# Cross-attention on one Trainium2 core: evener steps, a ring of four value chunks, output rows in one piece in the third step

## The chip, the cores and the metric

The kernel runs on one core of one Trainium2 chip. Its time is the device time of one execution in microseconds (us); lower is better. Engines are named as in the profile: PE is TensorE's matmul stream and PEld its weight loads, DVE is VectorE, ACT ScalarE, POOL GpSimd, SP SyncE, which issues most DMAs here.

## The reference

A pre-norm decoder layer on `x` of 32 x 112 x 512, float32, in three parts that each add to `x`: windowed self-attention, cross-attention to a context of 32 x 375 x 256, and an expert layer. The change is in the cross-attention alone:

```python
q = (layernorm(x) @ Wq)            # 16 heads of 128
k, v = ctx @ Wk, ctx @ Wv          # 8 key/value heads of 128, each used by two query heads
scores = einsum('bhtd,bhsd->bhts', q, k) / sqrt(128)
attn = softmax(where(mask, scores, -inf))
out = einsum('bhts,bhsd->bhtd', attn, v)
x = x + out @ Wo                   # 2048 -> 512
```

## The kernel before, in words

`cross_attention` does the heads in two halves (`HALVES`), so there are 64 pairs of a half and a batch, called batches 0 to 63 here (`b`); 0 to 31 are the first half. A batch has four steps (`g` 0 to 3, one key/value head and its two query heads each), 256 steps in all (`i = 4b + g`). Every product is made of matmuls on split numbers: a value is kept as a high part and a rest, and a product is three matmuls for each 128 of depth (high x rest, rest x high, high x high). So every tile that PE makes is read from PSUM twice: ACT copies the high part (`fill` at L1191, `probsT` at L1198, `out` at L1207), then DVE subtracts it and keeps the rest (`fill` at L1272, `probsT` at L1302, `out` at L1311).

In a step PE does, in this order (`@block.tensor`): the scores S of the step; the early fills, above all K, the keys of the same head for batch b+1; the product P of probabilities and values of two steps before; the late fills; the transposes T of the probabilities of the step before; the last late fill. The fills besides K are C (the context transposed, two per batch, first half only; it is written to DRAM and loaded again in the second half), V (the values, three chunks V0, V1, V2 of 128, 128 and 120 context rows), Q (the queries of four batches, eight fills, two in each step of every fourth batch, those with b mod 4 = 3) and O (the output rows, 24 matmuls for one tile of 128 rows, into which 28 of the 32 batches of a half bring one). Before the change C stands in step 3 ahead of P, all of V in step 1 around T, and O in step 2 ahead of P. All fills, O too, take PSUM banks in turn from `BANKS = 3`: a fill waits until DVE is through with the fill three places before it (`pe.wait_ge(fill_done, ...)` in `fill`).

The softmax of a step runs: DVE masks the scores and takes the maximum (`maxima`, L1295), POOL makes the bias (L1165), ACT the exponentials (L1215), DVE the inverse of the sum (`inverses`, L1320, L1323), POOL multiplies (L1171), PE transposes. ACT does in a step: weight splits, the K fill and C, the exponentials, a split of `xT` (input of Q, in the batches with b mod 4 = 1), `out`, `probsT` among the other fills. DVE: the mask row (step 0), `maxima`, weight splits, K and C, `inverses`, the `xT` split, the addition of the output rows (`add`, L1278), `out`, fills, `probsT`. Both engines take these in the written order, and a wait of one holds all behind it.

The context of a batch, the mask rows and the tiles of the residual are loaded by SP in one written order, and so are the weights, whose second half is loaded while the first is still in use (`splits_at` says in which steps they are split).

Of the kernel before, what the change touches and what calls it, by code (L numbers as in the profile page):

```python
# [16 lines left out]
P = 128  # L17
# [842 lines left out]
def cross_attention(nc, B, T, S, h2T, ctx, mask, Wq, Wk, Wv, Wo, base, mid, result):  # L860
# [19 lines left out]
    QUAD = 4  # L880
    T4 = QUAD * T
# [3 lines left out]
    RING = 2 * P  # L885
    SCALE = float(1.0 / np.sqrt(D))
    mdt = mask.dtype
    assert B * T % RING == 0 and B % QUAD == 0 and SE > S and T * 2 <= RING
# [9 lines left out]
    def early_fills(i):  # L898
        b, g = divmod(i, G)
        out = [("K", b + 1, g)] if b + 1 < NB else []  # L900
        if g == 3 and b + 2 < B:
            out += [("C", b + 2, 0), ("C", b + 2, 1)]
        if g == 2 and b in TILE_OF:
            out.append(("O", TILE_OF[b], 0))
        return out

    def late_fills(i):
        b, g = divmod(i, G)
        out = [("V", b, c) for c in range(NKC)] if g == 1 else []
        if b % QUAD == QUAD - 1 and b + 1 < NB:  # L910
            out += [("Q", b // QUAD + 1, 2 * g + h) for h in range(2)]
        return out

    def before_transposes(i):
        return late_fills(i)[:-1]

    def behind_transposes(i):
        return late_fills(i)[-1:]

    HEAD = [("C", 0, 0), ("C", 0, 1)] + [("K", 0, g) for g in range(G)] + [("C", 1, 0), ("C", 1, 1)] + \  # L920
           [("Q", 0, h) for h in range(H)]
    TAIL = ("O", TILE_OF[NB], 0)
    ORDER = HEAD + [f for i in range(STEPS) for f in early_fills(i) + late_fills(i)] + [TAIL]
    PLACE = {f: n for n, f in enumerate(ORDER)}
    assert len(PLACE) == len(ORDER)
    HALVED = {f: n for n, f in enumerate([f for f in ORDER if f[0] != "O"])}
    BANKS = 3
# [14 lines left out]
    PIECES = {"k": CC, "v": CC, "q": KC, "o": H // 2}  # L942
    FIRST_SPLITS = [("k", 0, n) for n in range(CC)], [("q", 0, n) for n in range(KC)], [("v", 0, n) for n in range(CC)]

    def splits_at(i):
# [3 lines left out]
        if b == B - 8 and g < CC:  # L949
            return [("k", 1, g)]  # L950
        if b == B - 3:
            return [("q", 1, g)]
        if i == G * B:
            return [("v", 1, n) for n in range(CC)]
        if b == B + 1:
            return [("o", 1, g)]
# [10 lines left out]
    def x_piece(i):  # L967

        b, g = divmod(i, G)
        return b // QUAD + 1 if b % QUAD == 1 and b // QUAD + 1 < NB // QUAD else None  # L970
# [3 lines left out]
    with ExitStack() as stack:  # L974
# [5 lines left out]
        wk = sb("wk", [P, HALVES, 2, CC, G * D], F32R)  # L980
# [5 lines left out]
        ctxn = sb("ctxn", [P, 2, NKC, CD])  # L986
        ctxT = sb("ctxT", [P, 2, 2, CC, SE], F32R)
        kT = sb("kT", [P, 2, G, SE], F32R)
        v = sb("v", [P, 2, NKC, G * D], F32R)
# [4 lines left out]
        mraw = sb("mraw", [T, 2, S], mdt)  # L994
# [27 lines left out]
        fill_ready, fill_hi, fill_done = sem("fill_ready"), sem("fill_hi"), sem("fill_done")  # L1022
        base_in = [sem(f"base_in{n}") for n in range(2)]
        stored = [sem(f"stored{n}") for n in range(2)]

        def weight(piece):

            kind, half, n = piece
            return [{"k": lambda: wk[:, half, a, n, :], "v": lambda: wv[:, a, n, :], "q": lambda: wq[:, a, n, :],
                     "o": lambda: wo[:, a, 2 * n:2 * n + 2, :]}[kind]() for a in (HI, LO)]  # L1030

        def weight_source(piece):
            kind, half, n = piece
            if kind in "kv":
                return (Wk if kind == "k" else Wv)[n * P:(n + 1) * P, half * G * D:(half + 1) * G * D]
# [1056 lines left out]
```

## Time and profile before

| | |
|---|---|
| median of 3 runs | 2684.8 us (2684.68 to 2687.51) |
| the profiled execution | 2685.35 us |
| its span | 2683.7 us |
| mean granted TensorE clock | 0.957 |
| PE busy | 2482.7 us (93%) |
| DVE busy | 1733.0 us (65%) |
| ACT, POOL busy | 1241.2, 1030.1 us |

The cross-attention takes from about 462 to 2395 us of the span. The page's busy shares are means over three stages; the views by line and the timeline tell more. In a timeline row stand the start, how long the run of equal instructions lasted, engine, line, operation and tiles; in brackets the engine's idle time before it and who ended it. Runs of matmuls overlap by the depth of the pipeline, so the distance between two starts, not the length, is what a run takes.

### The profile page before, as it was taken

Reading aid. Unit: us, or ns where it says so; the run is one execution under the profiler, and the core shown is the slowest. Engines: PE = TensorE matmul, PEld = TensorE weight load, DVE = VectorE, ACT = ScalarE, POOL = GpSimd, SP = SyncE. Lnnn points to the kernel's source line nnn. Section 1 sums busy time; section 2 is a strip of 40 time slices with the busy share of each in tenths; the row PEclk is TensorE's granted clock in tenths of the full one; section 3 lists DMA queues with packets and bytes.
Section 4 is the critical chain, followed back from the end, with each engine's and each line's share of the span. In section 5 each row is a group of like instructions: output and inputs, shape, how many; then the busy total and the mean of one; then the engine's idle time right before and its main releaser. Section 6 shows DMA issues by size and latency. Waiting matters only on the chain. (4 is left out here: it accounts for less than half of the span.)

```text
span 2683.7 us, 46237 instructions
## 1 busy us (share of the span) xinstructions
PE 2482.7 (93%) x14850; PEld 2257.6 (84%) x14851; DVE 1733.0 (65%) x4899; ACT 1241.2 (46%) x3183; POOL 1030.1 (38%) x1424
## 2 busy tenths in 40 slices
PE   6899897799999999999999999999999999979488
PEld 5888886788989898889989898898989888869376
DVE  7878886565575657566575756656565665644466
ACT  4555553454454545445454545445454454522211
POOL 4334443243343434334353534334343343431422
PEclk9999998899999999999999999999999999975699
DMA  8322332412122112212121211111111111122654
GB/s 256 95 71 84 96 108 89 162 50 66 62 75 66 62 54 74 74 52 83 52 91 58 88 55 53 54 41 55 51 57 54 53 55 41 41 72 70 220 178 129
DMA packets 108892, 217.87 MB, mean 81 GB/s; under 512 B 20336, under 2 KB 48720, under 8 KB 108416
## 3 DMA queue, kind: packets, MB, share of 16 engines
q1 hardware_dynamic: 103440, 188.42, 21.9%
q0 software_dynamic: 5040, 16.58, 1.7%
q10 hardware_dynamic: 224, 10.49, 1.2%
q8 instruction: 104, 1.70, 0.3%
q14 instruction: 84, 0.69, 0.1%
HBM read 134.57 MB, written 91.36 MB: 84 GB/s over the span
## 5 line engine op out<-in xcount | busy, mean ns | idle before, releaser
L1171 POOL TENSOR_SCALAR x_probs<-x_probs,x_inv 112x376 f32<-112x376 f32 x512 | 639.3, 1258 | 273.6 <-DVE x_inv L1323 273.6
L1165 POOL TENSOR_SCALAR x_bias<-x_top 112x1 f32<-112x1 f32 x512 | 129.1, 252 | 871.8 <-DVE x_top L1295 864.9
L1215 ACT ACTIVATE x_probs<-x_probs,x_bias 112x376 f32<-112x376 f32 x512 | 307.0, 603 | 105.2 <-POOL x_bias L1165 104.7
L1380 PE MATMUL x_ps_o<-x_pT,x_v 128*128 128x224 f32 (+1 forms) x2304 | 310.3, 279 | 43.2 <-DVE x_pT L1302 42.5
L1380 PEld LDWEIGHTS x_ps_o<-x_pT,x_v 128*128 128x128 f32 (+1 forms) x2304 | 288.0, 192 | 69.6 <-DVE x_pT L1302 61.5
L1380 PE MATMUL x_ps_f<-x_xT,x_wq 128*128 128x448 f32 x1536 | 339.3, 371 | 4.5 <-issue 4.5
L1380 PE MATMUL x_ps_f<-x_wo,x_oT 128*128 128x512 f32 x1344 | 315.7, 391 | 1.0 <-DVE x_oT L1311 1.0
L1380 PE MATMUL x_ps_s<-x_kT,x_qT 128*112 128x376 f32 x1536 | 314.6, 340 | 1.5 <-DVE x_top L1295 1.5
L1380 PE MATMUL x_ps_f<-x_ctxT,x_wk 128*128 128x376 f32 x1536 | 306.4, 335 | 1.9 <-DVE x_ctxT L1272 1.9
L1380 PEld LDWEIGHTS x_ps_f<-x_xT,x_wq 128*128 128x128 f32 x1536 | 282.4, 189 | 26.5 <-issue 4.7
L1380 PEld LDWEIGHTS x_ps_f<-x_wo,x_oT 128*128 128x128 f32 x1344 | 252.6, 189 | 50.0 <-issue 1.2
L1380 PE MATMUL x_ps_f<-x_wv,x_ctxT 128*128 128x512 f32 (+1 forms) x1152 | 290.7, 399 | 0.0
L1380 PEld LDWEIGHTS x_ps_f<-x_ctxT,x_wk 128*128 128x128 f32 x1536 | 269.4, 189 | 2.8 <-issue 1.6
L1295 DVE CUSTOM_DVE_ANT_0 x_probs<-x_ps_s,x_mrow 112x376 f32<-112x376 f32 x512 | 259.0, 543 | 11.1 <-DVE x_mrow L1283 11.1
L1380 PEld LDWEIGHTS x_ps_s<-x_kT,x_qT 128*112 128x112 f32 x1536 | 253.4, 175 | 10.0 <-issue 1.8
L1191 ACT ACTIVATE x_kT<-x_ps_f 128x376 fp32r<-128x376 f32 x256 | 124.1, 485 | 275.7 <-PE x_ps_f L1380 275.3
L1380 PEld LDWEIGHTS x_ps_f<-x_wv,x_ctxT 128*128 128x128 f32 (+1 forms) x1152 | 206.1, 187 | 43.1
L1302 DVE TENSOR_TENSOR x_pT<-x_ps_t,x_pT 128x336 fp32r<-128x336 f32 x512 | 234.2, 499 | 0.3 <-ACT x_pT L1198 0.3
L1207 ACT ACTIVATE x_oT<-x_ps_o 128x224 fp32r<-128x224 f32 (+6 forms) x352 | 93.7, 294 | 264.0 <-PE x_ps_o L1380 264.0
L1272 DVE TENSOR_TENSOR x_qT<-x_ps_f,x_qT 128x448 fp32r<-128x448 f32 x128 | 80.0, 625 | 208.7 <-ACT x_qT L1191 208.7
L1198 ACT ACTIVATE x_pT<-x_ps_t 128x336 fp32r<-128x336 f32 x512 | 202.1, 452 | 0.3 <-PE x_ps_t L1443 0.2
L1272 DVE TENSOR_TENSOR x_v<-x_ps_f,x_v 128x512 fp32r<-128x512 f32 (+1 forms) x192 | 132.5, 691 | 91.3 <-ACT x_v L1191 91.0
(186 smaller groups left out, 3799.5 us busy)
## 6 DMA issues: line engine op xcount, KB each, us to landing
x_ctxs<-x_ctxT SPq DMA_DIRECT2D x32, 752.0 KB, 3.8
x_ctxT<-x_ctxs SPq DMA_DIRECT2D x32, 752.0 KB, 4.3
x_xT<-h2T SPq DMA_DIRECT2D x16, 896.0 KB, 5.0
m_rows<-slots SPq DMA_DIRECT2D x35, 258.0 KB, 3.0
slots<-w_blank SPq DMA_DIRECT2D x8, 1032.0 KB, 5.2
x_ctxn<-in_ctx_dram SPq DMA_DIRECT2D x32, 256.0 KB
m_hn<-in_L_ffn_W_dram SPq DMA_DIRECT2D x32, 256.0 KB
w_xa<-in_x_dram SPq DMA_DIRECT2D x32, 224.0 KB, 3.3
```

Source lines behind the costliest of these rows:

```text
L1165: pool.tensor_scalar(bias[:, m:m + 1], top[:, m:m + 1], -0.1 * NEG, -SCALE, ALU.max, ALU.mult) \
L1171: pool.tensor_scalar(probs[0:T, m, 0:SE], probs[0:T, m, 0:SE], inv[:, m:m + 1], None, ALU.mult).then_inc(normed, 1)
L1191: act.activation(dst[HI], src, ACT.Copy).then_inc(fill_hi, 1)
L1198: act.activation(pT[:, HI, :, h * T:(h + 1) * T], ps_t[h][:, 0:NKC * T].rearrange("p (c t) -> p c t", c=NKC), ACT.Copy).then_inc(pT_hi, 1)
L1207: last = act.activation(oT[:, HI, 2 * g:2 * g + 2, at:at + t1 - t0], rows[:, :, t0:t1], ACT.Copy)
L1215: act.activation(probs[0:T, m, 0:SE], probs[0:T, m, 0:SE], ACT.Exp, bias=bias[:, m:m + 1], scale=SCALE, accum_out=total[:, m:m + 1]).then_ ...
L1272: dve.tensor_tensor(dst[LO], src, dst[HI].bitcast(F32), ALU.subtract).then_inc(fill_done, 1)
L1295: dve.tensor_tensor_reduce(out=probs[0:T, m, 0:SE], in0=ps_s[h][0:T, 0:SE], in1=mrow[:, i // G % 2, :], scale=1.0, scalar=-3.0e38, op0=ALU ...
L1302: dve.tensor_tensor(pT[:, LO, :, h * T:(h + 1) * T], ps_t[h][:, 0:NKC * T].rearrange("p (c t) -> p c t", c=NKC), pT[:, HI, :, h * T:(h + 1 ...
L1380: last = pe.matmul(out, w, r, start=m == 0, stop=m == len(jobs) - 1)
```

## The change

- Fills take their PSUM bank from two (`BANKS = 2`); the output rows leave the ring and have a bank of their own, `ps_r`, with counters of their own (`rows_ready`, `rows_added`). They still come in one piece in step 2 (`ROWS_AT = {2: [(0, H)]}`).
- V0 of batch b+1 moves to step 3 of batch b, so `v` becomes a ring of four chunks (`VRING`); V1 and V2 stay in step 1. C moves to step 2 (first of the two) and step 3, behind P.
- ACT does the exponentials first in a step, then K; DVE does `maxima`, then `inverses`, then K, then `out`, and only then `add`. The mask row moves to the end of step 1, the splits of weights and of `xT` to the end of a step; the `xT` splits now stand in steps 1 and 2 of the batches with b mod 4 = 1 and 2.
- One buffer instead of two for the context and the raw mask, and for `Wk`, which is cut in four pieces by heads instead of two by depth; `oT` holds three tiles of rows instead of two. SP's order is rewritten: in the head, `Wo` is loaded behind the second mask row, whose load waits for DVE's first `mask_row`; in the second half it is loaded behind the wait for V2 of batch 33.
- In the head, C of batch 1 moves between the fourth and the fifth Q fill, and V0 of batch 0 stands at the end.

```diff
-    RING = 2 * P
+    VRING = NKC + 1
+    RING = 3 * P
...
     def early_fills(i):
         b, g = divmod(i, G)
-        out = [("K", b + 1, g)] if b + 1 < NB else []
-        if g == 3 and b + 2 < B:
-            out += [("C", b + 2, 0), ("C", b + 2, 1)]
-        if g == 2 and b in TILE_OF:
-            out.append(("O", TILE_OF[b], 0))
-        return out
+        return [("K", b + 1, g)] if b + 1 < NB else []
 
     def late_fills(i):
         b, g = divmod(i, G)
-        out = [("V", b, c) for c in range(NKC)] if g == 1 else []
+        out = []
+        if g >= 2 and b + 2 < B:
+            out.append(("C", b + 2, g - 2))
+        if g == 3 and b + 1 < NB:
+            out.append(("V", b + 1, 0))
+        if g == 1:
+            out += [("V", b, c) for c in range(1, NKC)]
...
-    BANKS = 3
+    BANKS = 2
...
+    ROWS_AT = {2: [(0, H)]}
...
@@ scalar
                 for i in range(STEPS):
-                    for p in splits_at(i):
-                        split(p)
+                    exps(i)
                     for f in early_fills(i):
-                        if f[0] != "O":
-                            fill(f)
-                    exps(i)
-                    if x_piece(i) is not None:
-                        split_x(x_piece(i), i % G)
+                        fill(f)
...
@@ vector
                     maxima(i)
-                    for p in splits_at(i):
-                        split(p)
+                    inverses(i)
                     for f in early_fills(i):
-                        if f[0] != "O":
-                            fill(f)
-                    inverses(i)
...
                     if i >= 2:
                         out(i - 2)
+                    for tile, h0, h1 in row_parts(i):
+                        if h1 == H:
+                            add(tile)
```

PE, step 3 of a batch of the first half. The digit behind `x_ps_f` is the bank; `x_wk` marks K, `x_ctxn` C, `x_wv` V, `x_ps_s` S, `x_ps_o` P and `x_ps_t` T. Before:

```order
L1380 MATMUL x_ps_s0<-x_kT,x_qT 112x376 x3
L1380 MATMUL x_ps_s1<-x_kT,x_qT 112x376 x3
L1380 MATMUL x_ps_f2<-x_ctxT,x_wk 128x376 x6
L1392 MATMUL x_ps_f0<-x_ident,x_ctxn 128x128 x2
L1392 MATMUL x_ps_f0<-x_ident,x_ctxn 128x120
L1392 MATMUL x_ps_f1<-x_ident,x_ctxn 128x128 x2
L1392 MATMUL x_ps_f1<-x_ident,x_ctxn 128x120
L1380 MATMUL x_ps_o<-x_pT,x_v 128x224 x9
L1443 MATMUL x_ps_t0<-x_ident,x_probs 128x112 x3
L1443 MATMUL x_ps_t1<-x_ident,x_probs 128x112 x3
```

The same step after the change:

```order
L1410 MATMUL x_ps_s0<-x_kT,x_qT 112x376 x3
L1410 MATMUL x_ps_s1<-x_kT,x_qT 112x376 x3
L1410 MATMUL x_ps_f1<-x_ctxT,x_wk 128x376 x6
L1410 MATMUL x_ps_o<-x_pT,x_v 128x224 x9
L1422 MATMUL x_ps_f0<-x_ident,x_ctxn 128x128 x2
L1422 MATMUL x_ps_f0<-x_ident,x_ctxn 128x120
L1482 MATMUL x_ps_t0<-x_ident,x_probs 128x112 x3
L1482 MATMUL x_ps_t1<-x_ident,x_probs 128x112 x3
L1410 MATMUL x_ps_f1<-x_wv,x_ctxT 128x512 x6
```

One C has gone to the step before, the other stands behind P, and V0 ends the step in the bank that K had in the same step.

DVE, step 3 of the same batch. `x_kT`, `x_ctxT`, `x_v` are the rests of K, C, V; `x_sums` is `add`, `x_oT` is `out`, `x_pT` is `probsT`; `x_probs,x_top` and the `x_top` behind it are `maxima`, `x_total` and `x_inv` are `inverses`. Before:

```order
L1295 ISA x_probs,x_top<-x_ps_s,x_mrow 112x376
L1295 ISA x_top 112x1
L1295 ISA x_probs,x_top<-x_ps_s,x_mrow 112x376
L1295 ISA x_top 112x1
L1272 TENSOR_TENSOR x_kT<-x_ps_f,x_kT 128x376
L1272 TENSOR_TENSOR x_ctxT<-x_ps_f,x_ctxT 128x376 x2
L1320 TENSOR_SCALAR x_total<-x_total 112x1
L1323 RECIPROCAL x_inv<-x_total 112x1
L1320 TENSOR_SCALAR x_total<-x_total 112x1
L1323 RECIPROCAL x_inv<-x_total 112x1
L1311 TENSOR_TENSOR x_oT<-x_ps_o,x_oT 128x2x112
L1302 TENSOR_TENSOR x_pT<-x_ps_t,x_pT 128x3x112 x2
```

The end of step 2, from `add` on, and step 3 up to K after the change:

```order
L1307 TENSOR_TENSOR x_sums<-x_ps_r,x_sums 128x512
L1302 TENSOR_TENSOR x_ctxT<-x_ps_f,x_ctxT 128x376
L1331 TENSOR_TENSOR x_pT<-x_ps_t,x_pT 128x3x112 x2
L1324 ISA x_probs,x_top<-x_ps_s,x_mrow 112x376
L1324 ISA x_top 112x1
L1324 ISA x_probs,x_top<-x_ps_s,x_mrow 112x376
L1324 ISA x_top 112x1
L1349 TENSOR_SCALAR x_total<-x_total 112x1
L1352 RECIPROCAL x_inv<-x_total 112x1
L1349 TENSOR_SCALAR x_total<-x_total 112x1
L1352 RECIPROCAL x_inv<-x_total 112x1
L1302 TENSOR_TENSOR x_kT<-x_ps_f,x_kT 128x376
```

K has moved from ahead of `inverses` to behind them; `add`, which stood ahead of `out` in step 2, now stands behind it, with a C between it and `probsT`.

## Rows read from the trace of the kernel before

**Rows 1.** The page, part 1, the line of TensorE.

```profile
PE 2482.7 (93%) x14850; PEld 2257.6 (84%) x14851; DVE 1733.0 (65%) x4899; ACT 1241.2 (46%) x3183; POOL 1030.1 (38%) x1424
```

**Rows 2.** Waits of PE, 545 to 1420 us.

```profile
PE x_ps_o L1380 <- DVE x_pT L1302: 17.8, 23, 1.9
```

**Rows 3.** Waits of PE, 1420 to 2360 us.

```profile
PE x_ps_o L1380 <- DVE x_pT L1302: 18.6, 29, 1.8
```

**Rows 4.** Timeline of PE, end of batch 16 and start of 17.

```profile
1005.99 1.26 PE L1380 MATMUL x_ps_s<-x_kT,x_qT 128*112 128x376 f32 x6
...
1008.12 0.81 PE L1392 MATMUL x_ps_f<-x_ident,x_ctxn 128*128 128x128 f32 x6
1008.69 1.24 PE L1380 MATMUL x_ps_o<-x_pT,x_v 128*128 128x224 f32 x9
...
1010.28 1.27 PE L1380 MATMUL x_ps_s<-x_kT,x_qT 128*112 128x376 f32 x6
...
1012.42 1.17 PE L1380 MATMUL x_ps_o<-x_pT,x_v 128*128 128x224 f32 x9
...
1013.94 1.25 PE L1380 MATMUL x_ps_s<-x_kT,x_qT 128*112 128x376 f32 x6
...
1017.37 1.27 PE L1380 MATMUL x_ps_o<-x_pT,x_v 128*128 128x224 f32 x9 [1.16 <-DVE x_pT L1302]
1018.47 2.96 PE L1380 MATMUL x_ps_f<-x_wv,x_ctxT 128*128 128x512 f32 x12
```

**Rows 5.** Timeline of DVE, the same stretch.

```profile
1007.29 0.54 DVE L1295 CUSTOM_DVE_ANT_0 x_probs<-x_ps_s,x_mrow 112x376 f32<-112x376 f32 x1
...
1008.84 0.55 DVE L1272 TENSOR_TENSOR x_kT<-x_ps_f,x_kT 128x376 fp32r<-128x376 f32 x1 [0.53 <-ACT x_kT L1191]
1009.30 0.99 DVE L1272 TENSOR_TENSOR x_ctxT<-x_ps_f,x_ctxT 128x376 fp32r<-128x376 f32 x2
...
1012.85 0.55 DVE L1295 CUSTOM_DVE_ANT_0 x_probs<-x_ps_s,x_mrow 112x376 f32<-112x376 f32 x1 [0.17 <-DVE x_mrow L1283]
...
1015.56 0.63 DVE L1266 TENSOR_TENSOR x_xT<-x_xT 128x448 fp32r<-128x448 f32 x1
1016.11 0.38 DVE L1311 TENSOR_TENSOR x_oT<-x_ps_o,x_oT 128x224 fp32r<-128x224 f32 x1
1016.41 0.91 DVE L1302 TENSOR_TENSOR x_pT<-x_ps_t,x_pT 128x336 fp32r<-128x336 f32 x2
```

**Rows 6.** Timeline of ACT, the same stretch.

```profile
1008.32 0.49 ACT L1191 ACTIVATE x_kT<-x_ps_f 128x376 fp32r<-128x376 f32 x1 [1.56 <-PE x_ps_f L1380]
...
1014.97 0.56 ACT L1184 ACTIVATE x_xT<-x_xT 128x448 fp32r<-128x448 f32 x1
```

**Rows 7.** Groups by line: costs of single DVE operations, mean ns.

```profile
L1278 DVE TENSOR_TENSOR x_sums<-x_ps_f,x_sums 128x512 f32<-128x512 f32 x56 | 38.8, 692 | 187.9 <-PE x_ps_f L1380 187.9
```

**Rows 8.** Timeline of PE and DVE, step 3 of batch 15, a batch with Q fills.

```profile
976.29 1.19 PE L1380 MATMUL x_ps_s<-x_kT,x_qT 128*112 128x376 f32 x6
...
977.61 0.54 DVE L1295 CUSTOM_DVE_ANT_0 x_probs<-x_ps_s,x_mrow 112x376 f32<-112x376 f32 x1
```

**Rows 9.** Stretches of PE: us, busy (x), granted clock, DMA share, GB/s.

```profile
1487.00:1520.00 33.00, 28.64 (x193) 1.00 0.31 105
2355.00:2396.00 41.00, 34.14 (x182) 0.88 0.03 12
```

**Rows 10.** Timeline of DVE, first step.

```profile
511.90 1.29 DVE L1262 TENSOR_TENSOR x_wv<-x_wv 128x512 fp32r<-128x512 f32 x2
...
513.63 0.55 DVE L1295 CUSTOM_DVE_ANT_0 x_probs<-x_ps_s,x_mrow 112x376 f32<-112x376 f32 x1 [0.19 <-DVE x_mrow L1283]
```

**Rows 11.** Issue to landing of `Wo`, second half (tile x_wo, 1470 to 1520).

```profile
DMA to landing us min/median/max: 6.8/7.2/7.6
```

**Rows 12.** The same, first half (400 to 560).

```profile
DMA to landing us min/median/max: 10.6/10.9/11.3
```

**Rows 13.** The page, part 6: KB each, median us to landing.

```profile
x_ctxT<-x_ctxs SPq DMA_DIRECT2D x32, 752.0 KB, 4.3
```

More of the change, by code:

```diff
@@ L1007, in cross_attention @@
         ps_o = bank("ps_o")
+        ps_r = bank("ps_r")
         ps_f = [bank(f"ps_f{n}") for n in range(BANKS)]
@@ L1248, in _ @@
                         fill(f)
+                    if x_piece(i) is not None:
+                        split_x(*x_piece(i))
+                    for p in splits_at(i):
+                        split(p)
                 out(STEPS - 2)
@@ L1361, in _ @@
                         fill(f)
+                    if i % G == 1 and i // G + 1 < NB:
+                        mask_row(i // G + 1)
+                    if x_piece(i) is not None:
+                        split_x(*x_piece(i))
+                    for p in splits_at(i):
+                        split(p)
                 out(STEPS - 2)
@@ L1401, in fill @@
                                 pe.wait_ge(fill_done, until(("C", at, 1)))
-                        last = product(out[:, 0:SE], [(wk[:, half, a, c, n * D:(n + 1) * D], ctxT[:, at % 2, b_, c, :])
+                        last = product(out[:, 0:SE], [(wk[:, a, c, n * D:(n + 1) * D], ctxT[:, at % 2, b_, c, :])
                                                       for c in range(CC) for a, b_ in PASSES])
@@ L1414, in fill, with rows @@
                                                       for c in range(KC) for a, b_ in PASSES])
[L1415 to L1421 removed]
+                    last.then_inc(fill_ready, 1)
+                def rows(tile, h0, h1):
+                    if h0 == 0:
+                        weights("o", tile // TILES)
+                        pe.wait_ge(o_lo, G * (last_batch(tile) + 1))
+                        if tile:
+                            pe.wait_ge(rows_added, tile)
+                    slot = tile * P % RING
+                    for h in range(h0, h1):
+                        for a, b_ in PASSES:
+                            last = pe.matmul(ps_r[:], oT[:, a, h, slot:slot + P], wo[:, b_, h, :],
+                                             start=h == 0 and (a, b_) == PASSES[0],
+                                             stop=h == H - 1 and (a, b_) == PASSES[-1])
+                    if h1 == H:
+                        last.then_inc(rows_ready, 1)
                 def scores(i):
@@ L1463, in _ @@
                         fill(f)
+                    for tile, h0, h1 in row_parts(i):
+                        rows(tile, h0, h1)
                     if i >= 2:
@@ L1474, in _ @@
                 pv(STEPS - 1)
-                fill(TAIL)
+                rows(HALVES * TILES - 1, 0, H)
 def expert_ffn(nc, B, T, x2, wg, W, b, slots, out):
```

186 lines of the change are left out of this document (99 added, 87 removed).

## The prediction

> **What bounds the kernel now.** The first thing to read is the page's first part: PE is busy for 2482.7 of 2683.7 us [rows 1]. So the change can gain only what PE waits, or lose what it makes PE wait. It adds no matmul and takes none away. The list of waits of PE says what the cross-attention waits for: P for the probabilities that DVE halves last (L1302), 17.8 us in the first half and 18.6 us in the second [rows 2, 3]. Thirdly I read the timeline of a short stretch to see how these waits come about [rows 4 to 6]. PE takes 4.29 us for a step 3 (1005.99 to 1010.28) and 3.66 us for a step 0 (to 1013.94). DVE takes 5.56 us from the maxima of that step 3 to those of the step 0 (1007.29 to 1012.85), and its next `probsT` ends at 1017.32. Two short steps in a row let DVE fall behind, and the P of step 1 starts 1.16 us late, at 1017.37. The long steps (V, output rows) let DVE catch up. In three of four batches something of this is left; where the Q fills make every step long, nothing is.
>
> **The change part by part.** *Evening.* V0 lengthens step 3 by 1.45 us on PE (half of the 12 matmuls of 2.96 us, with their tail) [rows 4] and takes them from step 1. That is what the wait in step 1 needs, and taken alone it removes it.
>
> *How late DVE comes into step 3.* In the trace DVE starts the maxima at 1007.29, 1.30 us behind the start of the scores [rows 4, 5]. Now `add` (0.69 us, 0.62 of it not overlapped by its neighbour) [rows 7] no longer runs while DVE waits for ACT's `out`, but after it, and a C (0.99 us for two, 0.47 each) follows [rows 5]. The maxima start at 1007.29 + 0.62 + 0.47 = 1008.38. PE starts the scores later by one C only (half of 1008.69 - 1008.12), at 1006.27 [rows 4]. The lag grows from 1.30 to 2.1 us.
>
> *When K is free.* ACT now does K after both exponentials. In step 0 of the trace ACT is through with them and starts its next operation at 1014.97, 2.12 us behind DVE's maxima (1012.85) [rows 5, 6]. From ACT's start of K to DVE's start of K it is 0.52 us (1008.32, 1008.84), DVE takes 0.55, and PE follows 0.05 later (1017.32, 1017.37) [rows 4 to 6]. So K's bank is free 3.24 us behind the maxima: 1011.62.
>
> *The new wait.* The ring has two banks. In the first half step 3 fills them with K, C, V0, so V0 needs K's bank. PE is through with S, K, P, C and T of the step 4.29 us less one C after its start, and wants V0 at 1006.27 + 4.29 - 0.28 = 1010.28. V0 waits 1.3 us. Nothing of this is hidden: the scores of step 0 are queued behind V0 on PE, and DVE and POOL can't gain on it. In batches with b mod 4 = 1 or 2 an `xT` split (0.55 us, 1015.56 to 1016.11) [rows 5] now closes step 2 and delays the maxima: 1.9 us. With Q fills DVE comes 1.32 us behind PE into step 3 (976.29, 977.61) [rows 8], and V0 directly follows C: K is free at 4.56 us of the step, V0 wants to start behind scores and K (2.13), P (1.10, from 1017.37 to 1018.47) and one C (0.29) [rows 4], at 3.5: 1.1 us. Four batches: 1.3 + 1.9 + 1.9 + 1.1 = 6.2 us, and batches 2 to 29 are seven times four: **43 us**.
>
> *The old wait.* V0 ends 1.45 us after its release, DVE halves it and is 1.3 us behind PE in step 0; one short DVE step is now 4.2 us: 2.64 to the start of K, 0.46 for K, 0.30 for `out` (1016.11 to 1016.41), 0.83 for `probsT` (0.91 with its tail) [rows 5]. P of step 1 wants 3.66 + 2.14 = 5.8 us behind the start of step 0 [rows 4], the probabilities are there at 1.3 + 4.2 = 5.5. The old wait goes: **-17.8 us** [rows 2]. V2 in step 1 also takes K's bank. It wants it behind 2.13, P 1.10, V1 1.4 and T 0.5, 5.1 us into the step; DVE is 1.3 + 4.2 - 3.66 = 1.9 behind by then and frees it at 1.9 + 3.24: under 0.1 us, times 28 some **2 us**. In batches 9, 17 and 25 no output rows lengthen step 2, so on a lag of 2.1 us comes a DVE step of 4.7 against 3.95 on PE; P of step 3 wants its probabilities at 2.13 and has them at 2.8: 3 x 0.7 = **2 us**. First half: 43 - 17.8 + 2 + 2 = 29, **+29 us**.
>
> *Second half.* No C is made, so V0 follows K, and its bank is the one of K of step 2, long free. No V0 wait. But K has left the shadow in which DVE waited for the exponentials, and V0 adds 0.6 us of DVE to step 3. DVE enters step 3 with a lag of 1.9 us and needs 4.8 and 4.2 for steps 3 and 0, together 10.9; P of step 1 wants its probabilities at 5.1 + 3.66 + 2.14 = 10.9. So the wait is near 0.1 us, 0.65 where an `xT` split came before, and V2 waits 0.1 more: 0.2, 0.25, 0.8 and 0 in the four kinds of batches, 7.5 times 1.25 = 9 us. The four batches without rows add 1 us each: 13. Before it was 18.6 less the 4.4 of a stretch with weight splits (33.00 - 28.64) [rows 3, 9]: **-1 us**.
>
> *Weights at the half.* `Wo` now queues on SP behind the wait for V2 of batch 33, behind the copy of `ctxT` (752 KB, 4.3 us to land) [rows 13]. It lands 7.2 us after its issue if the copy doesn't hold it [rows 11], 11.5 if it does. DVE reaches the first split some 7 us after V2 (a lag of 2.1, a step of 4.2, an `xT` split of 0.55). With an issue or two ahead of it in the queue `Wo` is there after 8.5 to 12.5 us, so ACT and DVE stand 1.5 to 5.5 us; I take **+3 us**. The pieces of `Wk` come ahead of long steps: 0, covered by the output rows; at worst 3 us.
>
> *The head.* V0 needs the split of `Wv`, which DVE ends at 513.19 [rows 10]; the C that filled a gap adds 0.57. V0 then ends at 515.2, ACT and DVE halve it (0.6, 0.69), the mask row takes 0.44, and the first maxima start at 516.95 and not 513.63 [rows 7, 10]: 3.3 us. `Wo` is issued only when the mask row is done, and lands 7.2 us later [rows 11], 524.2; ACT is ready for it at 520.1. These 4.1 us nothing hides, since PE has only short steps there. With 0.5 us for K out of the shadow in three steps: **+9 us**. Bounds: the landing may be 10.9 us [rows 12], 13 in all; or only a few us in an empty queue, 4 in all. In these bounds lies also the 512-byte cut of `Wk`, two issues more ahead of the first context.
>
> *No cost.* `ps_r` makes `add` free of the ring, but the next fill doesn't wait for it before either. One buffer for context and mask: each is loaded at least a step 0 and a step 1 (3.7 + 6.7 us) ahead. Fewer `out`s are cut in two by the longer `oT`: a gain of some 3 us at most.
>
> **Sum.** 29 - 1 + 3 + 9 = 40 us on the profiled execution's own 2685.35: 2725.4 us. That execution is 0.5 us over the median of the runs, 2684.8, so I say 2725.
>
> The Trainium skill (Perfetto Trace Analysis, Optimizing Tensor Performance) has independent matmul groups rotate through different PSUM banks, so that the evacuation of one overlaps the next; it speaks against three banks made two. It gives no price; the sum by the rule alone is a V0 and V2 wait wherever the evacuation is late, which is what the rows give here.
>
> **Rivals.** *A: the evening works (faster).* K's bank is free in time, since PE is held elsewhere or ACT gets K in between. Then the waits of both halves go but for 2 us, -17.8 - 14.2 + 2 = -30, and the 12 us for head and half stay: 2667 us. It decides at a release of K less than 2.0 us behind the maxima, when the lag is 2.1. For it: the exponentials start earlier than before. Against it: ACT's order is fixed, and 2.12 us alone pass before it may touch K [rows 5, 6]. 0.11.
>
> *B: the wait is there but half as long*, because DVE's lag into step 3 stays 1.3 us (`add` and C find gaps): V0 waits 0.5, 1.1, 1.1 and 1.1 us in the four kinds, 27 us for 43: 2709 us. With a cheap head, 2704. For it: DVE has idle time between the exponentials. 0.13, inside the range.
>
> *C: gains and costs cancel*: V0 waits some 0.6 us in every batch, 17 us for 43, and the head costs 4 for 9: 2694 us, or a little less. 0.05.
>
> *D: TensorE's clock falls.* In the last steps, with 6.9 us of waits in 41, the granted clock is 0.88, and 1.00 in a stretch with 4.4 us in 33 [rows 9]. If each V0 wait cost the next 3.66 us step the lower level (1.2 for 2.4 GHz), 28 x 3.66 = 102 us more: 2827 us. Against it: waits of up to 1.9 us [rows 2] leave the clock at full level. The Trainium skill (TensorE: Matmul & The Clock Gate, A second HAM failure mode: psum-queue depth-cycling) tells of a kernel whose clock went up and down from short idle times while it cycled through PSUM banks; by that rule the rival would come true, and the trace so far doesn't agree. 0.03.
>
> **How the numbers follow.** The forecast has 0.68, its own range is 2710 to 2746: the V0 wait by 0.3 us either way is 8 us, the head -5 to +4, the half -1 to +3, `Wk` to +3. With B the range is 2696 to 2746; it leaves out A, most of C, D and the ends. Within 0.2%, 5 us, is about what a measurement of this kernel can tell from no change. Faster: A and a hundredth of C, 0.12; same: most of C, 0.04; slower: the forecast, B and D, 0.84.
>
> **What would show it.** In the profile after: a wait of PE for K's rest ahead of V0 (x_ps_f, released by DVE x_kT) in each batch up to 29, 1.1 to 1.9 us, and none in batches 32 to 63; the wait of P for the probabilities nearly gone in the first half and about the same in the second; DVE's maxima of step 3 starting 2.1 us behind the scores; the first maxima 3 us later and a wait of ACT for `Wo`. The prediction is wrong if V0 starts without a wait, if the second half changes by over 10 us, or if the head costs over 15.

## The result: slower by 1.9%, and the profile after

| | before | after |
|---|---|---|
| median | 2684.7 us | 2735.1 us (2731.9 to 2739.3) |
| ratio | | 1.0188, 95% interval 1.0173 to 1.0203 |
| span of the profiled execution | 2683.7 us | 2732.9 us |
| mean granted TensorE clock | 0.957 | 0.954 |

I predicted 2725 us and a range of 2696 to 2746. The page of the changed kernel, parts 1 and 5; behind the last bar stand the idle time of the engine ahead of the group and what ended most of it:

```profile
PE 2505.4 (92%) x14850; PEld 2265.1 (83%) x14851; DVE 1726.8 (63%) x4871; ACT 1227.2 (45%) x3155; POOL 1011.6 (37%) x1424
...
L1410 PE MATMUL x_ps_f<-x_wv,x_ctxT 128*128 128x512 f32 (+1 forms) x1152 | 312.7, 408 | 48.2 <-DVE x_kT L1302 45.7
```

The number of matmuls is that of [rows 1]. DVE, ACT and POOL have less to do than before, and the kernel is slower: what was added is waiting. Nearly all of the wait named stands ahead of V fills, for K's rest. PE's busy time is 22.7 us higher with equal work. Two things in the trace raise it, whose shares I have not worked out: where nothing waits, a run's recorded end overlaps the next run, and where one waits it doesn't; and the clock is low in places, shown below. So from here on I measure by distances between the starts of steps, not by the waits.

The waits of PE (us in total, times, longest), 545 to 1455 us, and 1455 to 2400 us:

```profile
PE x_ps_f L1410 <- DVE x_kT L1302: 41.0, 35, 2.6
PE x_ps_o L1410 <- DVE x_pT L1331: 1.9, 5, 0.7
```

```profile
PE x_ps_o L1410 <- DVE x_pT L1331: 9.6, 14, 1.3
PE x_ps_f L1410 <- DVE x_kT L1302: 3.9, 4, 1.3
```

In the first half the wait of P, 17.8 us before [rows 2], is nearly gone, and one of V0 for K's bank is there instead, in every batch. In the second half P waits 9.6 us where it waited 18.6 [rows 3] (8.8 us in the batches that [rows 3] cover).

PE in step 3 of batch 16, to the start of the next step 1. It answers to [rows 4]:

```profile
1038.52 1.26 PE L1410 MATMUL x_ps_s<-x_kT,x_qT 128*112 128x376 f32 x6
1039.62 1.19 PE L1410 MATMUL x_ps_f<-x_ctxT,x_wk 128*128 128x376 f32 x6
1040.65 1.22 PE L1410 MATMUL x_ps_o<-x_pT,x_v 128*128 128x224 f32 x9
1041.71 0.49 PE L1422 MATMUL x_ps_f<-x_ident,x_ctxn 128*128 128x128 f32 x3
1042.04 0.74 PE L1482 MATMUL x_ps_t<-x_ident,x_probs 112*128 112x112 f32 x6
1043.67 1.66 PE L1410 MATMUL x_ps_f<-x_wv,x_ctxT 128*128 128x512 f32 x6 [0.89 <-DVE x_kT L1302]
1045.16 1.18 PE L1410 MATMUL x_ps_s<-x_kT,x_qT 128*112 128x376 f32 x6
...
1048.72 1.26 PE L1410 MATMUL x_ps_s<-x_kT,x_qT 128*112 128x376 f32 x6
```

DVE in the same stretch, as [rows 5]:

```profile
1038.58 0.68 DVE L1307 TENSOR_TENSOR x_sums<-x_ps_r,x_sums 128x512 f32<-128x512 f32 x1
1039.18 0.54 DVE L1302 TENSOR_TENSOR x_ctxT<-x_ps_f,x_ctxT 128x376 fp32r<-128x376 f32 x1
...
1040.47 0.54 DVE L1324 CUSTOM_DVE_ANT_0 x_probs<-x_ps_s,x_mrow 112x376 f32<-112x376 f32 x1
...
1042.11 0.15 DVE L1349 TENSOR_SCALAR x_total<-x_total 112x1 f32<-112x1 f32 x1 [0.62 <-ACT x_probs L1245]
...
1042.89 0.16 DVE L1352 RECIPROCAL x_inv<-x_total 112x1 f32<-112x1 f32 x1
1043.06 0.55 DVE L1302 TENSOR_TENSOR x_kT<-x_ps_f,x_kT 128x376 fp32r<-128x376 f32 x1
```

The maxima start 1.95 us behind the scores, K's rest 2.59 us behind the maxima, and it is done at 1043.61. PE is through with the transposes and wants V0 at 1042.55 (the same transposes take 0.51 us to the next start wherever nothing waits). V0 starts at 1043.67: the step is 1.12 us longer, while the row's bracket says 0.89, since the transposes are recorded with 0.74 us. Between the maxima and the exponentials DVE stands idle for 0.62 us and then for 0.24, and K's rest, which could fill these gaps, comes behind them.

Where the 49.2 us of the spans went, from the starts of PE's steps (batches in the words ahead of the prediction):

| stretch | before | after | difference |
|---|---|---|---|
| start of the span to batch 2 | 553.6 | 572.9 | +19.3 |
| batches 2 to 29 | 841.3 | 871.9 | +30.7 |
| batches 30 to 34 | 142.9 | 148.9 | +6.0 |
| batches 35 to 62 | 817.8 | 814.5 | -3.3 |
| batch 63 to the end | 328.2 | 324.7 | -3.5 |

Of the head's 19.3 us the stage ahead gives 2.8: the first context transpose starts at 476.28 for 473.52, and this start lies anywhere from 472.6 to 478.6 in runs whose code up to there is the same. The other 16.5 are nearly twice what I had said. PE in the head, step 0 and 1 of batch 0, V0 to the scores of step 2:

```profile
517.97 1.64 PE L1410 MATMUL x_ps_f<-x_wv,x_ctxT 128*128 128x512 f32 x6 [2.58 <-DVE x_wv L1292]
...
526.14 0.74 PE L1482 MATMUL x_ps_t<-x_ident,x_probs 112*128 112x112 f32 x6
531.53 2.91 PE L1410 MATMUL x_ps_f<-x_wv,x_ctxT 128*120 128x512 f32 x6 [4.65 <-DVE x_kT L1302]
534.25 2.08 PE L1410 MATMUL x_ps_s<-x_kT,x_qT 128*112 128x376 f32 x6
```

V0 waits 2.58 us for the split of `Wv`; V2 of step 1 waits 4.65 us for K's rest, which stands on ACT and DVE behind a split of `Wo`. On ACT:

```profile
526.10 1.06 ACT L1210 ACTIVATE x_wo<-x_wo 128x1024 fp32r<-128x1024 f32 x1 [2.10 <-DMA x_wo<-own_wo]
```

V2 then takes 2.72 us to the next start instead of 1.49. The stretches of PE (us, busy, granted clock, DMA share, GB/s) say why:

```profile
531.00:537.00 6.00, 5.47 (x16) 0.52 0.79 276
546.00:551.00 5.00, 4.53 (x15) 0.66 0.59 184
600.00:1400.00 800.00, 768.34 (x4577) 1.00 0.21 65
```

### The profile page after: what moved, and what is told of

The parts are those of the page before. It is cut to its first block and busy times, and to the rows that moved or that the text cites. A ratio compares the mean times of both kernels' runs of the same rounds, so it can differ in the third digit from the quotient of the medians.

```text
span 2732.9 us, 46191 instructions
## 1 busy us (share of the span) xinstructions
PE 2505.4 (92%) x14850; PEld 2265.1 (83%) x14851; DVE 1726.8 (63%) x4871; ACT 1227.2 (45%) x3155; POOL 1011.6 (37%) x1424
## 5 line engine op out<-in xcount | busy, mean ns | idle before, releaser
L1195 POOL TENSOR_SCALAR x_bias<-x_top 112x1 f32<-112x1 f32 x512 | 117.2, 229 | 1015.6 <-DVE x_top L1324 1015.4
L1410 PE MATMUL x_ps_f<-x_wv,x_ctxT 128*128 128x512 f32 (+1 forms) x1152 | 312.7, 408 | 48.2 <-DVE x_kT L1302 45.7
L1410 PE MATMUL x_ps_o<-x_pT,x_v 128*128 128x224 f32 (+1 forms) x2304 | 304.8, 277 | 16.9 <-DVE x_pT L1331 16.9
L1456 PE MATMUL x_ps_r<-x_wo,x_oT 128*128 128x512 f32 x1344 | 314.3, 389 | 2.3 <-DVE x_wo L1292 1.4
L1456 PEld LDWEIGHTS x_ps_r<-x_wo,x_oT 128*128 128x128 f32 x1344 | 251.4, 188 | 51.1 <-DVE x_wo L1292 1.7
L1410 PEld LDWEIGHTS x_ps_s<-x_kT,x_qT 128*112 128x112 f32 x1536 | 259.3, 176 | 15.2 <-issue 1.8
L1340 DVE TENSOR_TENSOR x_oT<-x_ps_o,x_oT 128x224 fp32r<-128x224 f32 (+6 forms) x320 | 102.2, 336 | 211.9 <-ACT x_oT L1237 211.9
L1349 DVE TENSOR_SCALAR x_total<-x_total 112x1 f32<-112x1 f32 x512 | 78.8, 154 | 221.5 <-ACT x_probs L1245 221.5
```

The costliest lines, as they stand in the source:

```text
L1195: pool.tensor_scalar(bias[:, m:m + 1], top[:, m:m + 1], -0.1 * NEG, -SCALE, ALU.max, ALU.mult) \
L1340: last = dve.tensor_tensor(oT[:, LO, 2 * g:2 * g + 2, at:at + t1 - t0], rows[:, :, t0:t1], oT[:, HI, 2 * g:2 * g + 2, at:at + t1 - t0].bit ...
L1349: dve.tensor_scalar(total[:, m:m + 1], total[:, m:m + 1], 1e-30, None, ALU.max) \
L1410: last = pe.matmul(out, w, r, start=m == 0, stop=m == len(jobs) - 1)
L1456: last = pe.matmul(ps_r[:], oT[:, a, h, slot:slot + P], wo[:, b_, h, :], start=h == 0 and (a, b_) == PASSES[0], stop=h == H - 1 and (a, b_ ...
```

## The experiments

The question is which part of the change makes V0 wait, since three parts meet in that one wait: two banks instead of three, K behind the exponentials and inverses, and V0 in a step in which C also takes a bank. The theory is that it takes the first two together; the rivals, that one alone is enough, or that the place of C behind P makes it. The kernels ran in three groups, each on a chip of its own beside the kernel before: 2685.1, 2670.1 and 2671.5 us. The first group is `swap_vc`, `k_first`, `add_first` and `three_banks`, the third `k_act`, `k_dve` and `best3`; the changed kernel ran beside 2684.7 us. In the second and third group it takes 308 to 310 us from batch 63 to the end, for 323 to 326 in the first; the kernel before has no trace there, but its total is lower by about as much, 15 and 14 us. So I compare ratios, and PE's steps up to batch 63.

What was measured, in one place (stretches in us; "batch 2" and "batch 63" are where they start in the span):

| kernel | ratio (95% interval) | batch 2 | 2 to 29 | 30 to 34 | 35 to 62 | batch 63 |
|---|---|---|---|---|---|---|
| before | 1 | 553.6 | 841.3 | 142.9 | 817.8 | 2355.5 |
| after | 1.0188 (1.0173 to 1.0203) | 572.9 | 871.9 | 148.9 | 814.5 | 2408.2 |
| `swap_vc` | 1.0147 (1.0130 to 1.0164) | 568.0 | 864.7 | 148.9 | 814.5 | 2396.1 |
| `k_first` | 0.9927 (0.9911 to 0.9944) | 566.0 | 826.3 | 145.4 | 802.0 | 2339.6 |
| `add_first` | 1.0140 (1.0123 to 1.0157) | 572.0 | 863.0 | 149.0 | 812.0 | 2396.0 |
| `three_banks` | 0.9988 (0.9979 to 0.9998) | 564.6 | 832.1 | 149.1 | 809.5 | 2355.3 |
| `head` | 1.0145 (1.0128 to 1.0163) | 561.3 | 871.4 | 148.9 | 814.4 | 2395.9 |
| `v_step1` | 1.0023 (1.0014 to 1.0032) | 562.1 | 839.8 | 148.0 | 814.3 | 2364.2 |
| `three_k_first` | 0.9883 (0.9868 to 0.9898) | 565.7 | 819.3 | 146.4 | 800.0 | 2331.3 |
| `best` | 0.9884 (0.9866 to 0.9902) | 559.2 | 824.9 | 143.7 | 801.7 | 2329.4 |
| `k_act` | 1.0191 (1.0171 to 1.0211) | 576.0 | 872.9 | 147.6 | 816.6 | 2413.1 |
| `k_dve` | 1.0465 (1.0445 to 1.0485) | 575.1 | 899.0 | 155.5 | 853.8 | 2483.4 |
| `best3` | 0.9867 (0.9849 to 0.9885) | 559.8 | 817.9 | 146.3 | 799.6 | 2323.6 |

**Three banks.** The output rows go back into the ring:

```diff
-    BANKS = 2
+    BANKS = 3
...
-    ORDER = HEAD + [f for i in range(STEPS) for f in early_fills(i) + late_fills(i)]
+    ORDER = HEAD + [f for i in range(STEPS)
+                    for f in early_fills(i) + [("O", t, 0) for t, _, _ in row_parts(i)] + late_fills(i)] + [TAIL]
```

> The changed kernel with the output rows in the ring again and three banks for fills, everything else as it is. Theory 1: V0's bank is then that of the C of step 2, long free: the 39 us of waits ahead of V0 in the first half go, C and P wait a few us more: 2700 us, 2694 to 2708. Rival (lateness of DVE): 2720 or more.

2681.4 us, below my range. Batches 2 to 29 give back 39.8 us: step 3, in which V0 no longer waits, is 42.7 us shorter over the 28 batches, and the other steps are 2.9 longer. What is left of PE's waits, 545 to 1455 us, is the old one, 13.4 us for 1.9 after the change:

```profile
PE x_ps_o L1411 <- DVE x_pT L1332: 13.4, 21, 1.4
```

The total came out lower than expected because the head gave 8.3 us too (some 2 of them from the stage ahead) and the second half 5.0, where I had counted on no gain. So even there, with no V0 wait, two banks cost something.

**K first.** On both engines K is taken as soon as it is there:

```diff
@@ scalar
-                    exps(i)
                     for f in early_fills(i):
                         fill(f)
+                    exps(i)
@@ vector
-                    inverses(i)
                     for f in early_fills(i):
                         fill(f)
+                    inverses(i)
```

> The changed kernel with K ahead of the exponentials on ACT and ahead of the inverses on DVE again, two banks as they are. Theory 1: DVE is through with K 1.5 us behind its maxima and not 3.2, V0 waits 0 to 0.2 us, K is back in the time in which DVE waits for the exponentials, and the waits of P in the second half (9.6 us) go too: 2735 - 39 - 9 = 2687 us, 2682 to 2695. Rival (the early exponentials are worth something, since the chain scores, exponentials, transposes is what PE waits for): the gain is under half of it, over 2710 us.

2665.7 us: faster than the kernel before, and below my range. The theory holds for the wait (K's rest as a releaser of PE falls to 0.9 us in one place between 545 and 1455 us), but the gain is 69 us, and I had said 48. The V0 waits are some 39 of the 45.7 us of the first half, and the second half, which has no such waits, gives 12.5 more. DVE in step 3 of batch 16 of this kernel, and the first row of its next step:

```profile
1012.41 0.54 DVE L1324 CUSTOM_DVE_ANT_0 x_probs<-x_ps_s,x_mrow 112x376 f32<-112x376 f32 x1
...
1013.35 0.54 DVE L1302 TENSOR_TENSOR x_kT<-x_ps_f,x_kT 128x376 fp32r<-128x376 f32 x1
1014.05 0.15 DVE L1349 TENSOR_SCALAR x_total<-x_total 112x1 f32<-112x1 f32 x1 [0.16 <-ACT x_probs L1245]
...
1017.40 0.54 DVE L1324 CUSTOM_DVE_ANT_0 x_probs<-x_ps_s,x_mrow 112x376 f32<-112x376 f32 x1
```

K's rest starts 0.94 us behind the maxima (2.59 after the change) and lies in the time in which DVE waits for ACT anyway: that idle time is 0.16 us where it was 0.62. From these maxima to the next DVE takes 4.99 us, and 6.13 after the change (1040.47 to 1046.60; 1.12 of it V0's lateness).

**K first on one engine only.** Each half of the last edit by itself.

> K ahead of the exponentials on ACT alone; DVE still does the inverses, which wait for the exponentials, ahead of K's rest. Theory (the bank of K is free only when both engines have done K, so each order alone is enough to keep it late): DVE reaches K when the exponentials are through, and these are now later by K's 0.5 us. V0's wait stays at 1 to 1.7 us, the waits for x_kT between 560 and 1440 us stay at 30 to 50 us, and the start of batch 63 stays within 10 us of the 2408 us of the changed kernel; ratio 1.015 to 1.022. Rival (it was ACT that K kept busy at the wrong time, in the idle time it has ahead of the exponentials): most of the 69 us of both moves comes back, ratio under 1.003.

> K's rest ahead of the inverses on DVE alone; ACT still does the exponentials ahead of K. Theory: DVE waits for ACT's K at the same time as before, the bank is free earlier by the inverses alone (some 0.2 us of DVE), and these come that much later to POOL: V0's waits shrink by 0 to 0.3 us each, b 2 to 29 by 0 to 8 us; ratio 1.014 to 1.019. Rival (DVE's order alone decides): most of the 69 us comes back, ratio under 1.003.

`k_act` is as slow as the changed kernel, as expected, and `k_dve` is 2.7% slower still, which neither of its theories had. So neither engine's order alone decides; both must move. In `k_act` ACT has K's high part at 1045.57, in its idle time, but DVE takes K's rest at 1047.68, 2.50 us behind its maxima (1045.18), since the inverses are ahead. My expectation that the exponentials come later by K was off: they lose nothing. In `k_dve` DVE stands behind a K that ACT has not made yet, and now the inverses stand behind that, so they no longer lie in a gap. DVE, steps 0 and 1 of batch 17:

```profile
1063.09 0.54 DVE L1324 CUSTOM_DVE_ANT_0 x_probs<-x_ps_s,x_mrow 112x376 f32<-112x376 f32 x1
...
1065.69 0.55 DVE L1302 TENSOR_TENSOR x_kT<-x_ps_f,x_kT 128x376 fp32r<-128x376 f32 x1 [1.59 <-ACT x_kT L1221]
1066.16 0.14 DVE L1349 TENSOR_SCALAR x_total<-x_total 112x1 f32<-112x1 f32 x1
...
1067.78 0.54 DVE L1324 CUSTOM_DVE_ANT_0 x_probs<-x_ps_s,x_mrow 112x376 f32<-112x376 f32 x1
```

K's rest starts 2.60 us behind the maxima, exactly as after the change (1049.20 behind 1046.60), so V0's wait is the same 1.12 us. But DVE's short step takes 4.69 us instead of 4.20, so P and V2 wait in step 1. In the batches without Q fills it takes 7.9 to 8.2 us for 6.7 to 7.0 in the first half and 7.9 to 9.1 for 6.7 to 7.4 in the second. Batches 2 to 29 are 27 us longer than after the change, and 35 to 62 are 39 us longer. I had priced the inverses' delay by its own length and not asked what DVE's longer step brings to PE.

**Three banks and K first together**, to see whether the two causes add up.

> k_first and three banks with the output rows in the ring together. If V0's wait for K's bank was the whole cost of two banks, a third adds nothing once K is early: 2666 us, 2662 to 2669. If two banks cost elsewhere too (V2, K behind V0), it is faster, down to 2655.

Batches 2 to 29 take 819.3 us, 7.0 less than with two banks and K first. With the other three kernels this makes a square of the two causes:

| batches 2 to 29, us | K behind the inverses | K first |
|---|---|---|
| two banks | 871.9 | 826.3 |
| three banks | 832.1 | 819.3 |

A late K costs 12.8 us by itself, two banks 7.0 by themselves, and both together 52.6: 33 us belong to neither alone. They are the V0 wait less what it replaces: V0 waits 39.5 us in these batches only with both causes, and P's waits, 13.4 us with three banks and a late K, are then 1.9. By its ratio `three_k_first` is 12 us faster than `k_first`, about the most that my second case allowed; up to batch 63 it is 8.3 us. In the Trainium skill (Perfetto Trace Analysis, Optimizing Tensor Performance) matmul groups rotate through banks so that one's evacuation overlaps the next. The square agrees, and adds that what two banks cost here goes from 7.0 to 39.8 us with the time at which the evacuating engines come.

**V0 back in step 1**, on top of K first: the evening itself undone. V0 of batch 0 leaves the head too, by a line not shown.

```diff
-        if g == 3 and b + 1 < NB:
-            out.append(("V", b + 1, 0))
         if g == 1:
-            out += [("V", b, c) for c in range(1, NKC)]
+            out += [("V", b, c) for c in range(NKC)]
```

> k_first with all of V in step 1 again: K ahead of exponentials and inverses, two banks, C in steps 2 and 3, and no evening of V. If the evening is what gains (theory: PE's waits of P in step 1 come from two short steps in a row), the waits of P come back, some 15 us in each half, and the head gets 4 us cheaper for V0: 2666 + 30 - 4 = 2692 us, 2684 to 2698. If the gain of k_first came from the rest (C behind P, the two xT steps, fewer cut out's), it stays under 2675.

Against `k_first` the first half is 13.5 us longer and the second 12.4, and the ratio goes from 0.9927 to 1.0023: the evening is worth about 26 us on top of K first with two banks, and the 1.0023 lies in my range. It was not undone in any other kernel. My first-half reading was that it removes the 17.8 us wait of P. In `v_step1` P waits only 4.5 us, but another wait is there, of K's fill of step 0 for the C of step 3, whose context it reads: C stands behind P in this kernel, and no V0 lies between the two any more (545 to 1455 us):

```profile
PE x_ps_f L1408 <- DVE x_ctxT L1300: 13.6, 22, 1.6
PE x_ps_o L1408 <- DVE x_pT L1329: 4.5, 8, 0.8
```

**C behind V0** in step 3, so that V0 takes the bank that C had, and not K's:

```diff
-        if g >= 2 and b + 2 < B:
-            out.append(("C", b + 2, g - 2))
+        if g == 2 and b + 2 < B:
+            out.append(("C", b + 2, 0))
         if g == 3 and b + 1 < NB:
             out.append(("V", b + 1, 0))
+        if g == 3 and b + 2 < B:
+            out.append(("C", b + 2, 1))
```

> The changed kernel with V0 and C exchanged in step 3 of the first half: V0 stands ahead of T, C behind T, so C takes K's bank and V0 the bank of the C of step 2. Theory 1 (V0 waits for K's bank): PE's wait ahead of V0 (41.0 us for K's rest in 545 to 1455 us) goes; C, last in the step, waits 0.1 us in plain batches and 0.6 behind an xT split (10 us), and some waits of P for the probabilities come back (about 8 us), since DVE has C still to do: 2712 us, 2700 to 2718. Rival (DVE is simply too slow in step 3, the bank is only where it shows): the same total wait turns up elsewhere, 2725 to 2740.

A miss: 2723 us, and only 7.2 us less in batches 2 to 29. V0's wait is gone, but it has moved, not ended (waits of PE, 545 to 1455 us):

```profile
PE x_ps_f L1412 <- DVE x_ctxT L1304: 17.2, 23, 0.8
PE x_ps_f L1424 <- DVE x_kT L1304: 7.8, 16, 1.5
PE x_ps_f L1412 <- DVE x_v L1304: 6.6, 7, 0.9
```

C now waits for K's bank (7.8 us), and the K fill of the next step waits for C's rest (17.2). Not for the bank, which is V0's (6.6 us more), but for the data: this fill reads the context that C has just transposed, and C is now the last fill that is halved. I had looked at the banks alone. The order of three fills in two banks chooses who waits; it does not make DVE come earlier. C ahead of P, as before the change, was not run by itself; but `k_first` leaves C behind P, and V0 waits under 0.1 us in its batches 2 to 28, so that place alone does not make the wait.

**The addition ahead of `out`**, as before the change:

```diff
+                    for tile, h0, h1 in row_parts(i):
+                        if h1 == H:
+                            add(tile)
                     if i >= 2:
                         out(i - 2)
-                    for tile, h0, h1 in row_parts(i):
-                        if h1 == H:
-                            add(tile)
```

> The changed kernel with DVE's addition of the output rows ahead of `out` again. This measures the lag term by itself: DVE comes 0.6 us earlier into step 3 in the batches with output rows and without Q fills (18 of 28 in the first half), V0 waits 0.6 us less in each, 11 us, and P in the second half some 4 us less: 2720 us, 2716 to 2724. If the addition finds a gap in DVE anyway: 2733 to 2737.

2722.0 us, as expected: -8.9 us in batches 2 to 29, -2.5 in the second half. This was the term by which I let DVE's lag grow from 1.3 to 2.1 us (0.62 for the addition); K's rest as a releaser falls from 41.0 to 34.2 us.

**The head as before.** C of batch 1 ahead of the Q fills, the split of `Wv` ahead of the last Q fill, and `Wo` loaded ahead of the second mask row:

```diff
-           [("C", 1, 0), ("C", 1, 1)] + [("Q", 0, h) for h in range(4, H)] + [("V", 0, 0)]
+           [("Q", 0, h) for h in range(H)] + [("V", 0, 0)]
...
-                for f in HEAD[6:-1]:
+                for f in HEAD[6:-2]:
                     fill(f)
                 for p in FIRST_SPLITS[2]:
                     split(p)
-                fill(HEAD[-1])
+                for f in HEAD[-2:]:
+                    fill(f)
...
-                load_mask(1)
                 for n in range(PIECES["o"]):
                     load_w(("o", 0, n))
+                load_mask(1)
```

> The changed kernel with a mended head only: C of batch 1 directly behind the first K fills as before, the splits of Wv ahead of the last Q fill, and Wo loaded ahead of the second mask row. The profile after shows 1.9 us for C among the Q fills, 2.6 us of waiting for the split of Wv, 2.1 us of ACT waiting for Wo and a 4.7 us wait behind it that is followed by a low granted clock (0.52 in 531 to 537 us). If these are the causes, about 2 + 2.6 + 2.1 + 2 go: 2735 - 9 = 2726 us, 2722 to 2729, all of it before batch 2. If DVE and ACT bound the first steps whatever PE waits for (the splits of Wo), only 2 to 4 us go: 2731 to 2733.

Batch 2 starts 11.6 us earlier, 3.7 of them from the stage ahead: 7.9 for the head, where I expected 9. V0's wait for `Wv` is 0.15 us instead of 2.58, and V2 waits 2.65 us instead of 4.65, K's rest still being behind a split. PE, the head of this kernel:

```profile
510.48 1.64 PE L1412 MATMUL x_ps_f<-x_wv,x_ctxT 128*128 128x512 f32 x6 [0.15 <-DVE x_wv L1293]
...
522.05 1.65 PE L1412 MATMUL x_ps_f<-x_wv,x_ctxT 128*120 128x512 f32 x6 [2.65 <-DVE x_kT L1303]
523.54 1.20 PE L1412 MATMUL x_ps_s<-x_kT,x_qT 128*112 128x376 f32 x6
```

V2 takes 1.49 us again, and the granted clock stays at 1.00 there.

**The parts together.** `best` has K first, the addition first and this head, with two banks; `best3` has three banks too.

> k_first with the mended head and DVE's addition of the rows ahead of `out`: what the runs so far point to. The gains should add, since they lie at different places: 2666 - 8 (head, half of the clock loss being gone with K early) - 3 (9 us of waits of P are left, the lag explains a third): 2655 us, 2650 to 2661.

> Three banks with the output rows in the ring, K first on both engines, the addition ahead of out, and the changed head together. If the parts add up: from three banks with K first (batch 63 starts at 2331.3 us, ratio 0.9883) take the head and the addition (-10 by trace, as they gave on two banks with K first): batch 63 at 2321 us, ratio 0.9845 (0.983 to 0.987). Rival (the two-bank wait that is left there is the same wait that the addition and the head shorten, so they don't add): batch 63 at 2329 us or more, ratio 0.988.

`best` gave what was expected, a ratio of 0.9884. It is no faster than three banks and K first alone, since that has the 7.0 us of the third bank in place of the head's. `best3` has both: 0.9867, the fastest here, 36 us under the kernel before on its chip. Its ratio is in the range, but batch 63 starts at 2323.6 us, between the theory's 2321 and the rival's 2329: of 10 us some 8 came. But the first context transpose starts 2.5 us later in this run than in `three_k_first` (477.8 for 475.3 us); counted from there it is 10.2, so the parts add up. The addition gives only 1.4 in batches 2 to 29 once K is early. Its interval overlaps those of `best` and `three_k_first`, which ran on another chip, so that it beats these is shown by the steps of one profile each, not by the ratios.

## Why the prediction was right, and where it was not

The forecast was the first of my cases: the mechanism is the one named, in the place and with the sign that I gave, and the median lies 10 us over my number, in the range. The sum was 40 us and the spans grew by 49.2: the head is 7.5 over, the stage ahead gives 2.8, the first half 1.7 and the half 3.0 more than I had, and the second half (-2.3) and the end (-3.5) take some of it back. Step by step:

- *How late DVE comes into step 3*: 2.1 us predicted, 1.95 measured. `add_first` shows that the addition is a part of it.
- *When K is free*: 3.24 us behind the maxima predicted, 3.14 measured (1040.47 to 1043.61). V0 wanted 4.01 us into the step, 4.03 measured.
- *The new wait*: 1.3, 1.9, 1.9 and 1.1 us predicted. Measured by the distance from T to V0 (from C in batches with Q), less what it is without a wait: 1.12, 1.66, 1.66 and 1.2. Four batches have 5.6 us for 6.2, seven times four 39.5 for 43. `three_banks` gives back 39.8 and `k_first` takes this same wait away.
- *The old wait*: it was to go with its 17.8 us; 1.9 are left.
- *V2 and the batches without rows* were to cost 4 us. The rest of the first half, 30.7 - 39.5 + 15.9, is 7, from distances and recorded waits mixed; some 2.4 of it is the last step of batch 29 alone, where a weight split lengthens the wait to 2.56 us and the clock falls.
- First half: **+29** predicted, +30.7 measured. So this sum is right to 2 us, partly because the terms' errors balance.
- *Second half*: -1 predicted, -3.3 measured. Its reason, K out of the shadow and the evening nearly balancing, stands: with K early the same stretch is 12.5 us shorter, and with V0 back in step 1 all 12.4 are lost again. The wait of P was to stay about the same, and it halved: in batches 35 to 62 it is 6.6 us for 13.2 before. The steps together gained only half of that.
- *Weights at the half*: +3 for `Wo`. From step 0 of batch 33 to step 0 of 35 it is 48.4 us before and 51.8 after, +3.4; no run moved this load alone. `Wk` was put at 0 to 3: the rest of the stretch from batch 30 on, 2.6 us, holds step 0 of batch 30 at a low clock (5.1 us long, where a step 0 takes 3.6).
- *The head* is the term that was mis-sized: **+9** predicted, with bounds 4 and 13, and +19.3 measured, of which 2.8 are the stage ahead. The 16.5 left are over the 15 that I had named as a sign that the prediction is wrong: in this part it is. Three things were not in it. C among the Q fills takes two banks' turns: the fills wait, and C with its waits costs 2.1 us where I had 0.57 (the Q fills with C take 23.8 us to V0's turn, and 21.7 in `head`). A split that holds ACT and DVE holds K's rest too, and with two banks V2 and V0 wait for it, 4.65 and 2.24 us; I had counted the landing of `Wo` (4.1 us; ACT's wait for it is 2.10) once, as if only the split were late. And the low clock behind these waits costs another 4 us (V2 2.72 us and V0 2.28 for 1.49, the scores 1.88 and 1.80 for 1.0, a K fill 1.34 for 1.0). `head` takes away C's cost, the waits for `Wv` and `Wo` and this low clock, and gets 7.9 us back. Counted from the stage ahead, the first maxima come 5.0 us later, where I had 3.3.
- Batch 63 to the end: 3.5 us less, with no term for it. No run tells why; the changed kernels on the chip of the first group lie between 323 and 326 us here.

Of the rivals, *A* (the evening works) needed K's bank free within 2.0 us of the maxima: it is at 3.14, and `k_first`, where it is at 1.48, shows that the wait goes below the threshold and that the kernel is then faster than before; how exact the 2.0 is, no run shows. *B* (half the wait) falls by the lag of 1.95 us, where it had 1.3; *C* would have needed a still shorter wait. *D*, that the clock falls behind each V0 wait, did not come true in the steady batches: 1.00 from 600 to 1400 us with 1.1 to 1.7 us of wait each. But what I held against it was misread: waits of up to 1.9 us were to leave the clock at full level, and behind the longest of [rows 2], in batch 29 of the kernel before, it is low (PE, and a stretch of PE):

```profile
1374.06 2.25 PE L1380 MATMUL x_ps_o<-x_pT,x_v 128*128 128x224 f32 x9 [1.93 <-DVE x_pT L1302]
...
1374.00:1378.00 4.00, 3.94 (x15) 0.57 0.00 0
```

That D stayed away is therefore in part luck: how far the waits of 1.7 us are from a fall, no run shows. The rule from the Trainium skill on short idle times of a kernel that cycles through PSUM banks (TensorE: Matmul & The Clock Gate, A second HAM failure mode: psum-queue depth-cycling) is not borne out in the steady batches. In the head and at batch 29 the clock did fall, as D had it, but for single steps.

## What to carry to other kernels

When a ring of buffers is made smaller, ask for each fill when the *slowest reader* of the buffer it takes comes free, in the written order of that engine; two changes that cost 7 and 13 us alone cost 53 together, because one makes the buffer scarce and the other makes it come free late. (That is the first half; the second, which has no such fill, loses 12.5 us to the late K with two banks.) An operation that lies in an engine's idle time is free only in that place: K was free ahead of the exponentials and cost 69 us behind them (with two banks), and it must be moved on every engine in its chain, since moved on one alone it brought nothing on ACT and lost 2.7% more on DVE. In a head, where all steps are short, count a late weight once for the engine that splits it and again for each wait of PE behind it.

## What the runs showed of the hardware that was not expected

The granted clock fell behind some waits and not behind others of the same length. After the change it is at or near its lower level (1.2 for 2.4 GHz, a share of 0.50) in three places of the cross-attention once its steps run: at the 4.65 us in the head, at the 2.24 us that follow 15 us later, and at the 2.56 us in batch 29. The last of these, in stretches of PE:

```profile
1439.00:1443.00 4.00, 1.44 (x8) 0.79 0.00 0
1443.00:1447.00 4.00, 4.00 (x13) 0.50 0.77 258
```

With the changed head, waits of 2.65 and 2.24 us in the same two places leave it at 1.00 (stretches of PE around them):

```profile
519.00:523.00 4.00, 1.35 (x9) 1.00 0.71 233
522.00:527.00 5.00, 4.95 (x31) 1.00 0.04 10
535.00:540.00 5.00, 4.26 (x25) 1.00 0.54 163
```

So the length of the wait alone does not say whether the clock falls: a wait of 1.93 us was followed by a fall, and one of 2.65 was not. What else does stays open. Where it falls, the two or three runs of matmuls behind the wait take 1.6 to 2.8 us more.
